# A decoder on one core: one scan step a hop in norms and attention, three steps a chunk in the last mixtures

## What is computed

```
x = _layernorm(x + _L0_ffn_ref(x, ...))     # 8 experts, top 2, inner 256
x = _layernorm(x + _L1_attn_ref(x, ...))    # a scan over 512 positions (RWKV7), 16 heads of 16
x = _layernorm(x + _L1_xattn_ref(x, ctx))   # attention to a context of 512
x = _layernorm(x + _L1_ffn_ref(x, ...))     # 4 experts, top 2, and a shared one, inner 688
```

```
sa = einsum('bhij,bhj->bhi', S, a_t)
S  = S * exp(w_t) + sa[..., None] * b_t + v_t[..., None] * k_t
o_t = einsum('bhij,bhj->bhi', S, r_t)
```

## Time and profile before

| | us |
|---|---|
| median of 3 runs | 6065.13 (6060.26 to 6067.42) |
| the profiled execution | 6056.11 |
| its span, first to last instruction | 6054.3 |
| PE busy | 5506.3 (91%) |
| DVE busy | 3606.7 (60%) |
| ACT busy | 2103.8 (35%) |
| POOL busy | 317.7 (5%) |
| granted clock of TensorE, mean | 0.973 |

### The profile page before, as it was taken

How to read it: one execution, slowest core, us unless ns; L and a number is a source line. 1 busy time by engine, 2 the same in 40 slices (tenths; PEclk the granted TensorE clock), 3 DMA queues, 4 the chain that set the end, 5 groups by cost and what they waited for, 6 DMA issues and landing times. The chain is left out here.

```text
span 6054.3 us, 385300 instructions
## 1 busy us (share of the span) xinstructions
PE 5506.3 (91%) x171736; PEld 3879.1 (64%) x171736; DVE 3606.7 (60%) x16290; ACT 2103.8 (35%) x8003; POOL 317.7 (5%) x779
## 2 busy tenths in 40 slices
PE   6899999999999999999999999999888879887989
PEld 2577777777777777777777777777644444444433
DVE  4355555555555555555555555555487898888831
ACT  3144444444444444444444444444222122223221
POOL 0000000000000000000000000000011111111000
PEclk8999999999999999999999999999899899899989
DMA  1100000000000000000000000000211101011111
GB/s 69 57 2 2 2 2 2 2 2 2 2 2 2 2 2 2 2 2 2 2 2 2 2 2 2 2 2 17 81 58 40 40 28 47 31 45 33 47 38 54
DMA packets 45135, 111.64 MB, mean 18 GB/s; under 512 B 8160, under 2 KB 10208, under 8 KB 44528
## 3 DMA queue, kind: packets, MB, share of 16 engines
q1 hardware_dynamic: 43600, 109.39, 5.6%
q10 hardware_dynamic: 1440, 1.06, 0.1%
HBM read 99.90 MB, written 10.52 MB: 18 GB/s over the span
## 5 line engine op out<-in xcount | busy, mean ns | idle before, releaser
L711 PE MATMUL lstm_part_ps<-lstm_keys,lstm_hid 128*4 128x128 f32 x32768 | 1024.1, 273 | 205.5 <-DVE lstm_hid L880 205.5
L727 PE MATMUL lstm_ctx_ps<-lstm_values,lstm_alpha 128*4 128x128 f32 (+1 forms) x49152 | 1051.4, 237 | 0.2 <-issue 0.2
L711 PEld LDWEIGHTS lstm_part_ps<-lstm_keys,lstm_hid 128*4 128x4 f32 x32768 | 771.3, 86 | 427.2 <-DVE lstm_hid L880 413.6
L727 PEld LDWEIGHTS lstm_ctx_ps<-lstm_values,lstm_alpha 128*4 128x4 f32 x49152 | 904.8, 86 | 90.7 <-issue 0.4
L909 DVE TENSOR_REDUCE lstm_neg_max<-lstm_part_ps 128x1 f32<-128x128 f32 x1024 | 299.1, 292 | 678.8 <-PE lstm_part_ps L711 678.8
L842 ACT ACTIVATE lstm_expo<-lstm_part_ps,lstm_neg_max 128x128 f32<-128x128 f32 x1024 | 376.4, 368 | 862.2 <-DVE lstm_neg_max L909 862.2
L670 PE MATMUL lstm_half_ps<-lstm_w_hid,lstm_hid 128*13 128x96 f32 x16384 | 596.0, 246 | 0.0
L862 DVE STREAM_TRANSPOSE lstm_gates<-lstm_half_ps 128x96 f32<-128x96 f32 x1026 | 290.1, 283 | 396.1 <-PE lstm_half_ps L670 372.0
L670 PE MATMUL lstm_half_ps<-lstm_w_attn,lstm_attn 128*13 128x96 f32 x16448 | 526.0, 248 | 0.0
L670 PEld LDWEIGHTS lstm_half_ps<-lstm_w_attn,lstm_attn 128*13 128x13 f32 x16448 | 300.5, 93 | 154.6 <-ACT lstm_attn L855 106.7
L1944 ACT ACTIVATE mix_gated<-mix_gate_ps 115x512 f32<-115x512 f32 (+2 forms) x200 | 112.6, 563 | 820.0 <-PE mix_gate_ps L1674 819.9
(11 more groups left out here) (336 smaller groups left out, 8593.0 us busy)
## 6 DMA issues: line engine op xcount, KB each, us to landing
mix_ring<-in_sm_chunks SPq DMA_DIRECT2D x120, 358.0 KB, 2.9
mix_ring<-in_mix_chunks SPq DMA_DIRECT2D x80, 384.0 KB, 3.0
lstm_xg<-xg_rows SPq DMA_DIRECT2D x514, 16.0 KB
xg_rows<-lstm_xg_tile SPq DMA_DIRECT2D x16, 512.0 KB, 2.6
ctxT<-in_ctxT SPq DMA_DIRECT2D x1, 2048.0 KB, 14.6
out_xT<-xT SPq DMA_DIRECT2D x4, 512.0 KB, 3.8
xT<-in_xT SPq DMA_DIRECT2D x1, 1536.0 KB, 9.8
lstm_w_x<-in_lstm_w_x SPq DMA_DIRECT2D x1, 1024.0 KB, 10.8
```

Source lines behind the costliest of these rows:

```text
L711: mm = pe.matmul(part_rows(score_ps[part], b), hid[:, k, lo:lo + SPACE], keys[:, k, b * SRC + c * P:b * SRC + (c + 1) * P], start=(n == 0 ...
L727: mm = pe.matmul(part_rows(ctx_ps[n], b), alpha[:, b, c, SPACE - 1 - c:2 * SPACE - 1 - c], values[:, b * SC + c, ctx_cols[n]], start=(c == ...
```

## The change

Two numbers change, and what follows from them. `CHAIN_SLOTS = 1` takes the place of `SLOTS = 2` in attention (passed as `slots`) and in the norm behind every mixture. `CHUNK_SLOTS` becomes a pair for each mixture: (2, 3) for the first as before, (3, 3) for the last. Since the result on VectorE comes a step after the reciprocal in any case, the last pause of a norm is one step longer on TensorE and ScalarE, and VectorE's pause before the result is no longer one shorter than the others.

```diff
 SLOTS = 2
-CHUNK_SLOTS = (2, 3)
+CHAIN_SLOTS = 1
+CHUNK_SLOTS = {MIXTURE0: (2, 3), MIXTURE1: (3, 3)}
...
-            return 1 if slots == 1 or width < NB else CHUNK_SLOTS[n % 2]
+            return 1 if slots == 1 or width < NB else CHUNK_SLOTS[x.x][n % 2]
...
-                yield from attention(q, SLOTS)
+                yield from attention(q, CHAIN_SLOTS)
                 yield from mixture(SECOND, q, SLOTS)
...
                 down(count - 1)
                 yield from pause(slots)
                 pe.wait_ge(added, added_by_mixture(x, i) + 1)
                 ln.mean(pe, lambda k: token_block(x, i)[:, k, :], g.mean_mat[:, :], width)
-                yield from pause(slots)
+                yield from pause(CHAIN_SLOTS)
                 ln.variance(pe, norm_after_mixture(x, i), g.mean_mat[:, :], width)
-                yield from pause(slots)
+                yield from pause(CHAIN_SLOTS)
                 ln.spread(pe, norm_after_mixture(x, i), g.spread, width)
-                yield from pause(slots)
+                yield from pause(CHAIN_SLOTS + 1)
...
                 dve.tensor_tensor(block_x, down_ps[:, :, 0:width], block_x, ALU.add).then_inc(added, 1)
-                yield from pause(slots)
+                yield from pause(CHAIN_SLOTS)
                 ln.deviation(dve, norm_after_mixture(x, i), block_x, width)
-                yield from pause(slots)
+                yield from pause(CHAIN_SLOTS)
                 ln.inverse(dve, norm_after_mixture(x, i), width)
-                yield from pause(slots - 1)
+                yield from pause(CHAIN_SLOTS)
                 ln.result(dve, norm_after_mixture(x, i), block_x, width).then_inc(ln_done, 1)
...
                 ln.spread(pe, norm_after_attention(q), g.spread, width)
-                yield from pause(slots)
+                yield from pause(slots + 1)
```

More of the change, by code:

```diff
@@ L1507, in pause, with chunk_slots @@
             return (None for _ in range(n))
-        def chunk_slots(n, slots, width):
-            return 1 if slots == 1 or width < NB else CHUNK_SLOTS[n % 2]
+        def chunk_slots(x, n, slots, width):
+            return 1 if slots == 1 or width < NB else CHUNK_SLOTS[x.x][n % 2]
         slot = {}
@@ L1731, in mixture @@
                         router[x].turn_weights(pe, i, ident[:, :], tiles)
-                    yield from pause(chunk_slots(n, slots, x.width(i)))
+                    yield from pause(chunk_slots(x, n, slots, x.width(i)))
                 down(count - 1)
@@ L2277, in attention @@
                 ln.inverse(dve, norm_after_scan(q), width)
-                yield from pause(slots - 1)
+                yield from pause(slots)
                 ln.result(dve, norm_after_scan(q), block_x, width).then_inc(ln_done, 1)
```

## The result

The changed kernel takes 6096.76 us, the median of 5 runs (6093.06 to 6097.15); the kernel before, run beside it, 6062.28 (5 runs, 6058.66 to 6067.42). The ratio is 1.0054, 95% interval 1.0043 to 1.0065: **slower by 0.5%, some 34 us**. The profiled execution has a span of 6091.6 us against 6054.3, +37.3 (the first to the last instruction).

The account below looks back on a forecast made before the run. VectorE's chain of 512 scan steps bounds the kernel. Chunks −27, attention +24, norm chains +16, first mixtures with keys and values −8 sum to +5 us: 6061 profiled, 6070 as median; 8-in-10 range 6044 to 6096.

Parts of the forecast that it names:

- Rival 1: Slower: chains lose more than chunks win; attention waits 48 us, norm chains 26, sum +36, 6101 us; chance 0.24.
- own signs of being wrong: Part after the scan changing over 5 us, chunk waits staying over 50 us, or attention waits outside 20 to 45 us.
- The frame: In the scan, VectorE's work stays; the change wins or loses only VectorE's idle time there, 184.4 us.
- The count of hops: Whole scan: a block goes from 111 steps to 112, eight steps saved in first mixtures; 268.9 us after the scan stay.
- Attention: Attention blocks in the scan at one step a hop: waits from 8 to 32 us, loss 24, bounds 10 and 40.
- Block 1, 0 and 2: The scan's three attention blocks: waits of 4 us for block 1, 13 each for 0 and 2.
- The layout: Attention blocks 0 and 2: streams laid out with 13.3 us of projections in TensorE's queue, partly hidden, giving 13 us each.
- Norm chains: Six norm chains behind mixtures in the scan: waits from 3.5 to 20 us, loss 16, bounds 5 and 22.
- Chunks of the last mixtures: At three steps each, waits for the up projection fall from 62 to 35 us: gain 27, bounds 15 and 45.
- rival 3: No relief: three-step chunks idle TensorE, its clock drops, chunk waits stay near 50 us; +20, 6085 us; chance 0.09.
- First mixtures, keys and values: Their pieces shift two to six steps and a router's 9.6 us wait shrinks by 5.5: gain 8 us, bounds 0 and 15.

Follow-up runs that it names:

- x_shift: x_att with attention blocks held until scan steps 206, 302 and 430, so none begins in a tile's first steps; 17.3 us over x_att.
- x_att: The kernel before with only attention at one scan step a hop, norm chains and chunks as before; ratio 1.0028, +16.3 us.
- x_fill_after: The changed kernel with four unread matmuls behind last down projections, norm means and variances in steps 9 to 29 of a tile; ratio 1.0035 to the kernel before.
- x_norm: The kernel before with only the norm chains behind mixtures at one step a hop; ratio 1.0044, +27.6 us.
- x_norm_pad: x_norm with two empty steps behind each chain, so everything else keeps its step of the kernel before; ratio 1.0016, +10.8 us over the kernel before.

## Where the prediction was right and where wrong

The forecast was 6070; the time is 26.8 us over it and 0.8 over the upper end of the range. Beside its own kernel before, which ran 2.9 us faster than the one of the forecast, it is +34.5 where +5 was forecast. "Slower" had 0.35, "within 0.2%" 0.45. **Rival 1 is what happened**: it gave attention 48 us of waits (49.5 measured), a sum of +36 (the waits grew by 38.1) and 6101 us. Of the prediction's own signs of being wrong one came: attention waits outside 20 to 45 us. The scan is outside its 1443 ± 12, and two of the attention windows are longer than 60 us (61.2 and 63.7).

*The frame held.* VectorE's work in the scan is the same, and the loss is waits: 141.9 to 180.0, for a scan 37.7 us longer. The part behind the scan moved by 3.7 us, within the 5 allowed. The count of hops was right.

*Attention*, from 8 to 32 forecast, from 6.8 to 49.5 measured: **the step that failed**, 19 us of the miss. Block 1, 0 and 2: 4, 13 and 13, and 2 for the clock, against 9.1, 19.0 and 21.4. Three things were short. The layout let "the steps' own extra work hide part" of the projections; but in the empty steps of x_shift nearly all from 24 to 7 last 1.8 us, as bare ones do, and those from 8 to 23, there and in x_att, mostly 2 to 3; the work that hides is there, and x_att shows it (attention from step 4 waits 10.3 us, from step 0 21.9). The clock was taken at 2 us; x_fill_after takes 7 out of the attentions. And the projections were counted on TensorE alone; their followers on ScalarE, which the timeline of attention 2 shows inside the chain, had no term. The bound of a loss of 40 was too low as well, by 3 us. The argument against rival 1, that projections fall into TensorE's idle gaps, fails because they come at fixed steps and stand in front of the link that is due.

*Norm chains*, from 3.5 to 20 forecast, 21.6 measured: right for their own waits. But the steps that they save move all that follows. x_norm against x_norm_pad prices that at some 17 us where the chains alone are changed, and the sum had no term for it; how much of it is in the changed kernel, where everything stands in other steps again, no run shows.

*Chunks of the last mixtures*, −27 forecast, −21.4 measured: right in sign and mechanism. Most of the 6 us is likely half clock, costed at 3 us and 64 us long in the trace: in x_fill_after, with 44 us of it in the chunks, they wait 36.6 us, near the 35 forecast. That was rival 3's mechanism at a third of its price.

*First mixtures, keys and values*, −8 forecast, −1.5 measured. The router's wait shrank by more than was said (9.6 to 1.7, where 5.5 was forecast); the wait behind keys and values, 6.9 us, came in its place, and nothing in the prediction looked at ScalarE's queue there.

Why the sum is a loss and no trade: a two-step attention in a tile's first steps was cheap there (0.3 to 8.8 us, against 9 to 12 for a tile start full of chunks and about 20 for a one-step attention), since it needs little of TensorE. The change takes 12 steps from it and gives them to chunks that then leave TensorE idle outside the tile's first steps. TensorE's idle time in the scan is not reduced by it (197 to 204 us), only moved, and it brings 22 us of slower matmuls. Single parts: +16.3 and +27.6 for the two shortened chains, which leaves about −9 for the chunks; the intervals of the three ratios are 7 to 10 us wide to each side, so this −9 can't be told from nothing. The parts are not independent either: the chunks alone cost +51.8, since without the shorter attention 15 of them are left for the time behind the scan.

## What to carry to other kernels

Where background work runs beside a serial loop, cost it by the loop's own calendar: which steps carry foreign work in the queue of an engine that the chain needs (of each such engine: here TensorE and ScalarE), and which steps have work that covers a link. A hop that is shortened to one step is cheap in the latter and pays its whole latency in the former. Time that an engine stands idle in one place is not gained by pacing down another; check that its idle time as a whole falls, and price a shift of everything behind the edit as a term of its own.

## What the hardware showed that was not expected

Idle times of 1.90 and 2.87 us between TensorE's matmuls came with 10.2 us at half clock, in which the up projection took 3.75 us; and yet an idle time of 3.07 us in the kernel before came with none. The same instructions had 201 us at half clock in one scan and 218 in another, which was 3.6 us longer. And a clock restored by additional matmuls gives time only where TensorE is the one waited for: 72 us fewer at half clock left one scan as long as it was, 85 us took 14 from another, and 39 us took 4.5 from the bare chain behind the scan.
